# A recommendation tower in one kernel: both half batches of products first in each round, and gathers held until the first of them is done

## The reference

```python
e = jnp.stack([tbl_0[ids[:, 0]], ..., tbl_31[ids[:, 31]]], axis=1)   # 512 x 32 x 256
iu, ju = jnp.triu_indices(32, k=1)
z = jnp.einsum('bnd,bmd->bnm', e, e)[:, iu, ju]                      # 512 x 496
h = jnp.concatenate([z, dense_ctx], axis=1)                          # 512 x 512
h = jnp.maximum(h @ W_top1 + b_top1, 0.0)                            # 512 x 512
h = jnp.maximum(h @ W_top2 + b_top2, 0.0)                            # 512 x 256
y = h @ W_top3                                                       # 512 x 1
```

## Time and profile before

| what | value |
|---|---|
| median of 3 runs | 162.37 us (161.98 to 162.54) |
| span of the profiled execution | 231.2 us |
| mean granted clock of TensorE in it | 0.874 of full speed |
| PE busy with matmuls | 178.4 us, 77% |
| POOL busy (gathers) | 104.5 us, 45% |
| DVE, ACT busy | 95.2 us, 77.3 us |
| DMA | 26.77 MB, mean 116 GB/s |

### The profile page before, as it was taken

The page is one execution under the profiler, slowest core; times in us unless marked ns, Lnnn a source line. Parts: engine busy times, 40 slices in busy tenths (PEclk is TensorE's granted clock), DMA queues, the critical chain, the costliest instruction groups (busy, mean ns, idle before and its releaser), DMA issues.

```text
span 231.2 us, 6208 instructions
## 1 busy us (share of the span) xinstructions
PE 178.4 (77%) x2678; PEld 151.4 (66%) x2678; DVE 95.2 (41%) x311; ACT 77.3 (33%) x190; POOL 104.5 (45%) x110
## 2 busy tenths in 40 slices
PE   7999952999958889868494394929559295999995
PEld 6688831688946778757392392819458184899774
DVE  2896310836902859753116014220603232534331
ACT  3376413746843244113032051400304032234232
POOL 2777775565874445372417336360723614300000
PEclk9999995599995999999889559785958769799999
DMA  5999653577883345541303213130220303100000
GB/s 154 311 371 311 172 145 104 171 259 207 256 299 117 122 154 151 184 114 29 91 3 101 80 27 98 41 113 3 71 68 26 106 11 94 45 6 4 4 6 0
DMA packets 12869, 26.77 MB, mean 116 GB/s; under 512 B 2917, under 2 KB 3881, under 8 KB 12842
## 3 DMA queue, kind: packets, MB, share of 16 engines
q0 software_dynamic: 4992, 13.64, 19.9%
q1 hardware_dynamic: 7706, 12.47, 16.5%
q10 hardware_dynamic: 144, 0.26, 0.5%
HBM read 26.36 MB, written 0.00 MB: 114 GB/s over the span
## 4 chain that ended last, share of the span: by engine, by line
PE 65%; issue 21%; ACT 9%; another core or an unknown queue 2%; DVE 1%; POOL 0%; POOLq 0%
PE bank L614 18%; PE bank L565 14%; PE bank L621 13%; PE xt_ps L584 11%; ACT high L450 3%; PE bank L648 3%; ACT kept L458 3%; PE bank L674 2%; ACT xt L463 2%; PE xt_ps L701 2%; PE xt_ps L674 1%; DVE pairs L394 1%; PE bank L682 1%; ACT h L496 0%
## 5 line engine op out<-in xcount | busy, mean ns | idle before, releaser
L346 POOL DMA_INDIRECT rows<-table,row_ids x104 | 103.8, 998 | 94.7 <-PE xt_ps L584 62.1
L614 PE MATMUL bank<-xt 128*32 128x32 f32 (+1 forms) x1664 | 45.2, 219 | 36.9 <-issue 36.0
L614 PEld LDWEIGHTS bank<-xt 128*32 128x32 f32 (+1 forms) x1664 | 35.0, 129 | 47.8 <-issue 44.1
L463 ACT COPY xt<-xt_ps 128x512 f32<-128x512 f32 (+1 forms) x43 | 22.2, 554 | 85.3 <-PE xt_ps L584 75.2
L394 DVE COPY pairs<-bank 32x64 f32<-32x64 f32 (+1 forms) x184 | 39.6, 215 | 12.7 <-PE bank L614 10.4
L377 DVE COPY xt<-xt_ps 128x512 f32<-128x512 f32 (+1 forms) x14 | 9.2, 654 | 84.8 <-PE xt_ps L584 84.8
L584 PE MATMUL xt_ps<-ident,rows 128*128 128x128 f32 x208 | 33.4, 306 | 7.1 <-issue 5.0
L565 PE MATMUL bank<-one_hot,high 128*128 128x512 f32 (+1 forms) x128 | 31.8, 369 | 2.2 <-issue 1.2
L621 PE MATMUL bank<-pairs,w_sb 128*128 128x128 f32 x192 | 32.2, 329 | 1.2 <-issue 1.2
L584 PEld LDWEIGHTS xt_ps<-ident,rows 128*128 128x128 f32 x208 | 26.7, 157 | 9.6 <-issue 5.9
L366 DVE TENSOR_SCALAR one_hot<-small_ids_sb,first_sb 128x512 fp32r<-128x512 int32 (+1 forms) x64 | 24.5, 422 | 17.4 <-remote 11.8
(11 more groups left out here) (36 smaller groups left out, 44.8 us busy)
## 6 DMA issues: line engine op xcount, KB each, us to landing
small_sb<-small_tables SPq DMA_DIRECT2D x31, 256.0 KB
w_sb<-w SPq DMA_DIRECT2D x8, 256.0 KB
rows<-table,row_ids POOLq DMA_INDIRECT x104
small_ids_sb<-small_ids SPq DMA_DIRECT2D x3, 256.0 KB
small_ids_sb<-small_ids SPq DMA_DIRECT2D x4, 128.0 KB
w_sb<-w SPq DMA_DIRECT2D x1, 512.0 KB, 5.6
small_ids_sb<-small_ids ACTq DMA_DIRECT2D x1, 256.0 KB
small_sb<-small_tables SPq DMA_DIRECT2D x2, 128.0 KB, 3.5
```

Source lines behind the costliest of these rows:

```text
L346: nc.gpsimd.indirect_dma_start(rows[:, i % ROWS, :], None, table, bass.IndirectOffsetOnAxis(ap=row_ids[:, i:i + 1], axis=0)).then_inc(gath ...
L463: nc.scalar.copy(*fill_parts(f)).then_inc(xt_act, 1)
L614: done = nc.tensor.matmul(dots_ps[later(n)][n % 2][quads, g, :], x, x, start=(c == 0), stop=(c == DC - 1))
```

## The change

In each round both halves of the products come first, then layer 2, layer 3, layer 1, look-ups and fills; the two tables for layer 1 become one, `LAYER1_IN`, with the same pieces in the same rounds. Each half of a unit's products now increments a semaphore, the first `dots_half_done`, the second `dots_done`. POOL's wait ahead of a gather whose slot was freed by fill e is as before, and where e is a fill of round r, POOL also waits until the first half of the products of round r+1 is done.

```diff
-LEAD_LAYER1 = {5: (0, [0]), 6: (0, [3]), 7: (0, [6]), 9: (1, [0]), 10: (1, [3]), 11: (1, [6]), 13: (2, [0, 1]),
-               14: (2, [4, 5])}
-TRAIL_LAYER1 = {5: (0, [1, 2]), 6: (0, [4, 5]), 7: (0, [7]), 9: (1, [1, 2]), 10: (1, [4, 5]), 11: (1, [7]),
-                13: (2, [2, 3]), 14: (2, [6, 7])}
+LAYER1_IN = {5: (0, [0, 1, 2]), 6: (0, [3, 4, 5]), 7: (0, [6, 7]), 9: (1, [0, 1, 2]), 10: (1, [3, 4, 5]),
+             11: (1, [6, 7]), 13: (2, [0, 1, 2, 3]), 14: (2, [4, 5, 6, 7])}
+        dots_half_done = sem("dots_half_done")
         dots_done = sem("dots_done")
+        def round_of(f):
+
+            return next(r for r in range(ROUNDS) if f in fills_in(r))
+
                 if fill_gathers(f)[-1] >= ROWS:
 
-                    pool.wait_ge(transposed, next(e for e in range(f) if fill_gathers(f)[-1] - ROWS in fill_gathers(e)) + 1)
+                    e = next(e for e in range(f) if fill_gathers(f)[-1] - ROWS in fill_gathers(e))
+                    pool.wait_ge(transposed, e + 1)
+                    if e >= EARLY:
+
+                        pool.wait_ge(dots_half_done, round_of(e) + 2)
-                if groups[-1] == GROUPS - 1:
-                    done.then_inc(dots_done, 1)
+                done.then_inc(dots_half_done if h == 0 else dots_done, 1)
             for r in range(ROUNDS):
+                dots(2 * r)
+                dots(2 * r + 1)
                 if r in LAYER2_IN:
                     layer2_of(LAYER2_IN[r])
                 if r in LAYER3_IN:
                     layer3(LAYER3_IN[r], l3_ps)
-                if r in LEAD_LAYER1:
-                    b, halves = LEAD_LAYER1[r]
+                if r in LAYER1_IN:
+                    b, halves = LAYER1_IN[r]
                     for i in halves:
                         layer1_half(b, i)
-                dots(2 * r)
-                if r in TRAIL_LAYER1:
-                    b, halves = TRAIL_LAYER1[r]
-                    for i in halves:
-                        layer1_half(b, i)
-                for two in twos_in(r)[:1]:
-                    look_up(two)
-                dots(2 * r + 1)
-                for two in twos_in(r)[1:]:
+                for two in twos_in(r):
                     look_up(two)
                 for f in fills_in(r):
```

## The result

The kernel after takes **167.02 us** (166.77 to 168.82, 4 runs) beside 162.45 for the one before: a ratio of 1.0295, 95% interval 1.0238 to 1.0352. That is 4.6 us or 2.8% slower. The forecast was slower too, but by 1.95, and the range ended at 166.6: the sign was right, the size was not, and the time lies just outside the range.

What follows compares the result with a forecast made beforehand. The kernel was taken as bound by gathers from about round 7 to the end of round 13, then by PE. Terms 0.95 + 0.8 + 0.2 + 0 = +1.95 us on 162.37 gave 164.3; range 159.6 to 166.6.

Steps and rivals of the forecast that it cites:

- base sum: Kernel before, from undisturbed profile rows: PE's work and POOL's gathers, round 14 ending at 145.0, span at 157.7 us.
- unexplained 4.7 us: Median above the summed end of 157.7: what lies around the span and what PE or POOL are slower by.
- (1): Products first in a round: PE waits for fill copies, counted as 0.2, 0.8 and 0.95 us in rounds 12 to 14.
- (2): Products ahead of look-ups and layers: relu1 and kept tables come nearer to ACT's copies; nothing, up to 0.5 us.
- (3): POOL's new wait for the first half of products: 0 us, hidden by its backlog of gathers; bound 1.8.
- Rival C: Slower by more: without a backlog on POOL the new wait's delays of 1.8 reach the end; 166.6 us, chance 0.15.
- (4): Gathers no longer beside products: removes most of the profiled stall; worth 0 to 4.7 us in runs, taken as 0.
- Rival A: Faster: stalls of products beside gathers are partly real; 159.6 to 161.8 us, chance 0.28.
- (5): Semaphore and bookkeeping: one increment more per half batch and some fifteen waits on POOL; nothing.
- the feed of instructions: Supply of instructions: named only as something that may lie outside the range, without a size.
- The rule that I weighed: Matmuls start no closer than about 25 ns: second 64 products of rounds 6 to 14, +8 us, left to slower tail.

Runs made afterwards that it cites:

- e0_before: The kernel before, unchanged, run again for a second profile: 162.44 us, ratio 1.0047.
- e7_split: The kernel after without the new wait on POOL, and with the second half of the products behind layers and look-ups: 163.35 us, ratio 1.0074.
- e2_wait_only: The kernel before with the new wait on POOL and its semaphore, old order on PE: 163.26 us, ratio 1.0024.
- f1_64_columns: The kernel after with products of units 6 to 15 two samples (64 columns) at once, 64 matmuls a unit instead of 128: 164.94 us, ratio 1.0079.
- f2_old_from_12: The new order in rounds 0 to 11, the old one in rounds 12 to 14, no new wait on POOL: 162.78 us, ratio 1.0002.
- e1_order_only: The kernel after without the new wait on POOL: 167.1 us, ratio 1.0307.
- e5_before_pad34: The kernel before with 34 small matmuls (136 instructions) more in the warm-up: 164.72 us, ratio 1.0183.

## Why the prediction was wrong, point by point

**The base sum** held well, though it was built from the undisturbed parts of a disturbed profile. It put the 104th gather at 136.1 (137.8 in `e0_before`), a landing at 3.5 us (median 3.4 there, 4.1 after), the end of round 14 at 145.0 (147.8) and the span at 157.7 (160.6). Of the unexplained 4.7 us 1.8 lie around the span and 2.9 are real. One step was off: in that profile PE waits for a gather for the last time in round 10, at 116.31, so rounds 11 to 13 are bound by PE already and not by gathers. Part of it is the price of the products: half a batch was put at 0.69, and while gathers run, in rounds 12 and 13, it takes 0.87 to 0.99 at the upper clock level.

**(1), the copy waits.** The mechanism and the rounds were right. From the start of the last transpose to the start of the first product it is 0.56, 0.95 and 0.95 us in rounds 12, 13 and 14, forecast as 0.5, 0.95 and 0.95. The prediction calls these numbers idle, and reads 0.8 as the idle ahead of the last products, where the earlier trace rows has 0.56: the step includes the last transpose itself, and the idle is 0.29, 0.67 and 0.68. As rounds 12 and 13 are bound by PE, all of it counts in the profiled execution: 2.46 less three ordinary steps, 2.1 with 0.1 for a step (transposes to a layer, as the old order has it) and 1.9 with 0.2 (transposes to products, as in rounds 8 to 10 of the kernel after). The measured price by `e7_split` is 1.2 (0.4 to 2.0).

**(2)** nothing: no PE idle behind relu1 or the kept tables from round 12 on; in round 11, idle of 0.3 ahead of the products of round 12 is in (1).

**(3), the new wait on POOL,** costs nothing that can be told, as forecast: `e2_wait_only`, 1.0024, with no wait on POOL of over 0.3 us. Rival C, which would have given 166.6 by it, was close in time by luck and wrong in cause.

**(4)** was rightly taken as zero. Rival A rested on stalls beside gathers: the profile of `e0_before` has nothing of the kind though POOL issues all the time, and its ten runs take 161.9 to 164.3.

**The step that failed is the paragraph behind (5),** the feed of instructions. I read 128 products in a row at 10 ns each with no gap, and the sum has no term for products that run out of instructions. That row shows the rate while instructions are there; it says nothing of whether they are. The page of the kernel before had the 21 packets of 16 KB all along, and a unit of products is 256 instructions, one whole packet. The prediction names the feed only as what may lie outside the range, without a price. By `f1_64_columns` it is the larger part of the loss. In the one profile of the kernel after, the path from the last wait for a gather to the last products has over `e0_before`:

- stop in round 11, 2.0, and layer 1 at the lower clock behind it, 3.34 instead of 1.98 on the chain: 1.4;
- stop in round 14: 1.3;
- copy waits: 2.1;
- less what before has there and after has not, two pieces of layer 1 at the lower clock behind the 1.68 us wait for a gather, 1.62 and 1.70 instead of 1.06: -1.2.

The sum is 5.6, the path was 5.1 longer, and the tail behind is 0.3 shorter than before (a stop behind the last products of 0.72 instead of 1.00). Against the forecast of 1.95, the 4.6 of the runs leave some 2.6 us for the feed and the clock; by `f1_64_columns` it is 3.5. The split between rounds is that of one profile: `f2_old_from_12` has the stop of round 11 without losing time in its median, and `e1_order_only` is as slow as the kernel after with the clock at its upper level.

The rule that I weighed, matmuls no closer than about 25 ns (the Trainium skill, "TensorE: Matmul & The Clock Gate", "Wait — 56ns, not 53.3ns?"), is not what happened: 128 products take 1.89 us, 15 ns each, in round 12, with no gap. The page that bears on it is another. The Trainium skill ("Runtime: NRT & Kernel Launch", "Instruction fetch mechanics") says that instructions are fetched in blocks of 16 KB or 256 instructions, which the traces here show exactly, and that this is hidden because the sequencer is slower than the fetch. That second part does not hold here: 256 instructions were used in 1.86 us, and the restart comes 1.2 to 1.6 us after the end of a packet that itself takes 0.9 to 1.4 at the stops.

## What to carry to other kernels

Small matmuls can use up instructions faster than a fetch brings them. At the stop of round 14 the next block could be used 3.4 us after PE had entered the one before, and the instructions in hand lasted 1.86. So count a burst of small matmuls against the block, and put longer instructions (layers, look-ups) between a semaphore wait and the burst; the order that does so here had no long stop and lost nothing that could be told. A change of order can cost through this without any work or wait being added, and a few instructions anywhere ahead of it move the place. And when a profile's span doesn't fit the runs, take a second profile before reading stalls from it.

## What the runs showed that I had not expected

- PE stands still at numbers 193 + k*256 of its recorded instructions and goes on 1.2 to 1.6 us after the end of a packet of 16 KB; the longest was 2.7 us from the last instruction to the next, in `e5_before_pad34`.
- Halving the number of instructions at more PE time made the kernel faster: 1.0079 (0.9961 to 1.0198) for 64 columns, 1.0295 (1.0238 to 1.0352) for 32.
- The stalls of the first profile (67 matmuls in 10 us) did not come again in any of the profiles after it. What caused them stays open.
- What sets the start of a block's fetch, and whether gathers on the same DMA engines make it later, was not tried.
